# Moving one weight split to VectorE and narrowing the last chunk by column halves in a graph-attention block

## The reference, cut to what matters

```
h   = relu(layernorm(x))                        # x: 2048 x 256
hs  = layer_norm(h) * ln1 ; ht = layer_norm(h_target) * ln1
q, k, v = ht @ Wq, hs @ Wk, hs @ Wv             # 8 heads of 32
probs = softmax(where(adj != 0, q @ k.T, -1e30)) # 2048 x 2048 for each head
ht  = ht + (probs @ v) @ Wo + bo
ht  = layer_norm(ht) * ln2                      # the "y" of the kernel
ff  = gelu(ht @ W1) @ W2                        # W1: 256 x 1024, W2: 1024 x 256
out = x + ht + ff
```

## Time and profile before

| | |
|---|---|
| runs shown | 508.99, 513.01, 1082.84 us; median 513.01 |
| profiled execution | 511.34 us, span of the core's instructions 509.7 us (1.64 us lie outside) |
| mean granted TensorE clock | 0.992 |
| busy | PE 476.3 us (93%), DVE 420.1 (82%), ACT 391.1 (77%), POOL 310.0 (61%) |
| stretches | attention until about 395 us, mixing until 406.6, feed-forward until 503.2, tail until 509.7 |

### The profile page before, as it was taken

The page is one execution under the profiler, slowest core; times in us unless marked ns, Lnnn a source line. Parts: engine busy times, 40 slices in busy tenths (PEclk is TensorE's granted clock), DMA queues, the critical chain, the costliest instruction groups (busy, mean ns, idle before and its releaser), DMA issues.

```text
span 509.7 us, 10621 instructions
## 1 busy us (share of the span) xinstructions
PE 476.3 (93%) x4364; PEld 244.4 (48%) x4364; DVE 420.1 (82%) x626; ACT 391.1 (77%) x467; POOL 310.0 (61%) x153
## 2 busy tenths in 40 slices
PE   3899979999999899999899999999999799999995
PEld 1466623333333333333333333333335688888884
DVE  5688589999998999999999999999997787565252
ACT  4787978998998898998899998899896371627250
POOL 1000009995997997998998999899999500000000
PEclk9899999999999999999999999999999999999999
DMA  8998399722642851322762400160000100202021
GB/s 255 246 205 151 89 250 402 251 42 51 201 78 38 119 123 37 70 42 44 90 164 42 86 1 2 32 181 1 2 1 2 44 11 33 84 0 84 0 84 44
DMA packets 53232, 46.95 MB, mean 92 GB/s; under 512 B 35454, under 2 KB 46108, under 8 KB 52668
## 3 DMA queue, kind: packets, MB, share of 16 engines
q1 hardware_dynamic: 50672, 37.30, 27.4%
q0 software_dynamic: 2480, 8.92, 10.1%
q10 hardware_dynamic: 28, 0.01, 0.0%
HBM read 31.93 MB, written 14.81 MB: 92 GB/s over the span
## 4 chain that ended last, share of the span: by engine, by line
PE 49%; ACT 18%; DVE 17%; issue 8%; POOL 4%; DMA 3%; DVEq 0%; POOLq 0%
DVE probs L994 11%; ACT probs L721 10%; PE acc L1335 9%; PE slot L1320 8%; ACT maskT L654 4%; PE acc L1353 4%; PE slot L1435 3%; PE slot L1433 3%; PE slot L1434 3%; PE acc L1450 3%; PE acc L1448 3%; PE acc L1449 3%; PE slot L1233 3%; PE slot L1251 2%; POOL added_up L528 2%
## 5 line engine op out<-in xcount | busy, mean ns | idle before, releaser
L994 DVE SCALAR_TENSOR_TENSOR probs<-maskT,slot 128x1024 f32<-128x1024 bf16 x256 | 298.8, 1217 | 14.9 <-PE slot L1320 14.4
L721 ACT ACTIVATE probs<-probs 128x1024 f32<-128x1024 f32 x256 | 261.1, 1053 | 21.9 <-DVE probs L994 11.0
L528 POOL TENSOR_TENSOR added_up<-added_up,probs 128x1024 f32<-128x1024 f32 x96 | 226.7, 2396 | 1.7 <-ACT probs L721 1.6
L1335 PE MATMUL acc<-probs,V 128*32 128x512 f32 x1024 | 137.2, 608 | 7.1 <-ACT probs L721 7.1
L1353 PE MATMUL acc<-probs,ones 128*32 128x256 f32 x1024 | 77.0, 379 | 0.0
L1320 PE MATMUL slot<-q_hi,k_hi 32*128 32x512 f32 x512 | 64.9, 496 | 7.6 <-DVE probs L994 7.6
L1353 PEld LDWEIGHTS acc<-probs,ones 128*32 128x32 f32 x1024 | 33.3, 110 | 72.8 <-issue 71.2
L525 POOL TENSOR_TENSOR added_up<-probs 128x1024 f32<-128x1024 f32 x16 | 38.0, 2391 | 44.5 <-ACT probs L721 24.4
L1320 PEld LDWEIGHTS slot<-q_hi,k_hi 32*128 32x128 f32 x512 | 24.6, 182 | 65.7 <-DVE probs L994 54.0
L781 ACT ACTIVATE g_full<-slot 128x512 f32<-128x512 f32 x32 | 19.2, 600 | 45.3 <-issue 30.8
L1320 PE MATMUL slot<-q_lo,k_hi 32*128 32x512 f32 x512 | 52.0, 392 | 0.0
(11 more groups left out here) (132 smaller groups left out, 512.2 us busy)
## 6 DMA issues: line engine op xcount, KB each, us to landing
adj_raw<-in_adj POOLq DMA_DIRECT2D x16, 512.0 KB, 5.3
xs<-in_x SPq DMA_DIRECT2D x4, 512.0 KB, 6.9
htn<-in_L_gnn_h_target SPq DMA_DIRECT2D x4, 512.0 KB, 7.0
ht_saved<-htn SPq DMA_DIRECT2D x1, 2048.0 KB, 7.6
k_hi_saved<-k_hi SPq DMA_DIRECT2D x1, 2048.0 KB, 10.6
k_lo_saved<-k_lo SPq DMA_DIRECT2D x1, 2048.0 KB, 14.1
v_saved<-V SPq DMA_DIRECT2D x1, 2048.0 KB, 9.4
inverse<-inverse_saved SPq DMA_DIRECT2D x8, 256.0 KB
```

Of the source, the lines that this page charges most:

```text
L528: nc.gpsimd.tensor_tensor(added_up[:, pair], added_up[:, pair], at(i), ALU.add).then_inc(added, 1)
L721: nc.scalar.activation(p, p, ACT.Exp).then_inc(exped, 1)
L994: nc.vector.scalar_tensor_tensor(out=probs[:, u % RING], in0=m, scalar=MASKED if c else CEILING, in1=slot[u % SLOTS][:], op0=ALU.add, op1= ...
L1335: mm = pe.matmul(acc[HD * j:HD * j + HD, 0, :], V[:, i, h * HD:(h + 1) * HD], probs[:, (PAIRS * k + j // 2) % RING, j % 2, :], start=(i == 0),
```

## The change

It has three parts.

1. The subtraction that makes `w2_lo` leaves POOL and becomes one DVE instruction, `split_second_weight`, right behind `y_apply(0)` and ahead of `add_residual(2)`.
2. POOL's last residual: its first step waited for the norm of chunk 0 (`norm_y`), its second for `yT_lo` of chunk 0 (`y_lo_out`). Both now stand behind `y_lo_out`.
3. The last chunk's narrowing becomes `narrow_last`: all eight blocks f for the columns 0 to 127 first, then all for 128 to 255. The first half is joined, transposed (into `slot[0]`, behind the fifth block of the second half) and finished while the second half runs; the second half is joined in two pieces of 256 rows, each transposed and finished by itself. SP waits for the counts that this gives.

```diff
--- before.py
+++ after.py
@@ -452,7 +452,7 @@
             for c in range(NCH):
                 for half in range(2):
                     ts = slice(half * TILES // 2, (half + 1) * TILES // 2)
-                    sp.wait_ge(summed, TILES * c + (half + 1) * TILES // 2)
+                    sp.wait_ge(summed, TILES * c + (half + 1) * TILES // 2 + (TILES if c == LAST else 0))
                     sp.dma_start(out_rows[:, rows_of(c), :][:, ts, :], result[:, ts, :]).then_inc(stored, 16)
                 if c < LAST:
                     sp.dma_start(xr[:], x_rows[:, rows_of(c + 1), :]).then_inc(x_again, 16)
@@ -569,12 +569,9 @@
                         nc.gpsimd.tensor_tensor(w1_lo[:], w1_raw, w1_hi[:].bitcast(F32), ALU.subtract
                                                 ).then_inc(w1_lo_made, 1)
 
-            pool.wait_ge(w2_hi_made, 1)
-            nc.gpsimd.tensor_tensor(w2_lo[:], w2_raw, w2_hi[:].bitcast(F32), ALU.subtract).then_inc(w2_lo_made, 1)
-
-            pool.wait_ge(norm_y, LN2)
+
+            pool.wait_ge(y_lo_out, DC)
             make_residual(LAST, 0)
-            pool.wait_ge(y_lo_out, DC)
             make_residual(LAST, 1)
 
             general = load_flag(pool, "pool")
@@ -1067,6 +1064,37 @@
                     nc.vector.scalar_tensor_tensor(out=result[:, t, :], in0=acc4[:, t, :], scalar=nodes[:, n:n + 1],
                                                    in1=xr[:, t, :], op0=ALU.mult, op1=ALU.add).then_inc(summed, 1)
 
+            def finish_last():
+                def join_part(d, at, width):
+                    ts = slice(at, at + width)
+                    nc.vector.tensor_tensor(out_T[:, d, ts], acc[:, d, ts], yT[LAST % 2][:, d, ts], ALU.add
+                                            ).then_inc(joined, 1)
+
+                def result_part(t, d):
+                    n, ds = LAST * TILES + t, slice(d * P, (d + 1) * P)
+                    nc.vector.scalar_tensor_tensor(out=result[:, t, ds], in0=slot4[0][:, t, ds], scalar=nodes[:, n:n + 1],
+                                                   in1=xr[:, t, ds], op0=ALU.mult, op1=ALU.add).then_inc(summed, 1)
+
+                dve.wait_ge(out_turned, 2 * LAST)
+                dve.wait_ge(narrowed, DC * LAST + 1)
+                join_part(0, 0, CHUNK)
+                dve.wait_ge(x_again, 16 * NCH)
+                dve.wait_ge(stored, 32 * LAST)
+                dve.wait_ge(out_turned, 2 * LAST + 1)
+                for t in range(TILES):
+                    result_part(t, 0)
+                dve.wait_ge(narrowed, DC * NCH)
+                for half in range(2):
+                    join_part(1, half * CHUNK // 2, CHUNK // 2)
+                for half in range(2):
+                    dve.wait_ge(out_turned, 2 * LAST + 2 + half)
+                    for t in range(half * TILES // 2, (half + 1) * TILES // 2):
+                        result_part(t, 1)
+
+            def split_second_weight():
+                dve.wait_ge(w2_hi_made, 1)
+                nc.vector.tensor_tensor(w2_lo[:], w2_raw, w2_hi[:].bitcast(F32), ALU.subtract).then_inc(w2_lo_made, 1)
+
             def divide_last():
                 dve.wait_ge(inverses_in, 16 * GROUPS * NCH)
                 dve.wait_ge(context_out, GROUPS * NCH)
@@ -1088,6 +1116,7 @@
             y_stats(0)
             y_root(0)
             y_apply(0)
+            split_second_weight()
             add_residual(2)
             turned_y_lo(0)
             add_residual(1)
@@ -1115,10 +1144,11 @@
                     find_largest()
                 else:
                     make_flag()
-                join(c)
+                if c < LAST:
+                    join(c)
                 if c == 0:
                     add_residual(LAST)
-            finish(LAST)
+            finish_last()
 
             general = load_flag(dve, "dve")
             with dve.If(general):
@@ -1435,6 +1465,28 @@
                         mm = pe.matmul(dst, w1_lo[:, d, fs], yT_hi[:, d, :], start=False, stop=(d == DC - 1))
                     mm.then_inc(widened, 1)
 
+            def narrow_last():
+
+                pe.wait_ge(summed, TILES * LAST)
+                for d in range(DC):
+                    for f in range(FC):
+                        pe.wait_ge(gelu_lo, LAST * FC + f + 1)
+                        ds, dst = slice(d * P, (d + 1) * P), acc[:, d, :]
+                        pe.matmul(dst, w2_hi[:, f, ds], g_hi[:, f, :], start=(f == 0), stop=False)
+                        pe.matmul(dst, w2_hi[:, f, ds], g_lo[:, f, :], start=False, stop=False)
+                        mm = pe.matmul(dst, w2_lo[:, f, ds], g_hi[:, f, :], start=False, stop=(f == FC - 1))
+                        if d == 1 and f == FC // 2:
+                            pe.wait_ge(joined, DC * LAST + 1)
+                            for t in range(TILES):
+                                turned_mm = pe.transpose(slot4[0][:, t, 0:P], out_T[:, 0, t * P:(t + 1) * P], ident[:])
+                            turned_mm.then_inc(out_turned, 1)
+                    mm.then_inc(narrowed, 1)
+                for half in range(2):
+                    pe.wait_ge(joined, DC * LAST + 2 + half)
+                    for t in range(half * TILES // 2, (half + 1) * TILES // 2):
+                        mm = pe.transpose(slot4[0][:, t, P:D], out_T[:, 1, t * P:(t + 1) * P], ident[:])
+                    mm.then_inc(out_turned, 1)
+
             def narrow(c):
                 if c == 0:
                     pe.wait_ge(w2_lo_made, 1)
@@ -1470,10 +1522,12 @@
                 else:
                     pe.wait_ge(largest_made, 2 * NCH + 1)
                     pe.transpose(slot[2][0:1, 0, 0:P], largest_all[:], ident[:]).then_inc(largest_turned, 1)
-                narrow(c)
+                if c < LAST:
+                    narrow(c)
+                else:
+                    narrow_last()
                 if c == 0:
                     attend(LAST)
-            turn_out(LAST)
 
             general = load_flag(pe, "pe")
             with pe.If(general):
```

## The result

The changed kernel takes 506.36 us in the median of 18 executions, the one before 511.33 of 18. The ratio of the undisturbed executions is 0.9916 with a 95% interval of 0.9893 to 0.9939, which is 4.3 us less (3.1 to 5.5). The forecast was 508.1 us, 3.3 less. Executions that a disturbance made far longer than the rest (here 1082.84 us of before and 512.75 of the changed kernel) stay in the medians of this document and are left out of its ratios.

What follows compares the result with a forecast made beforehand. PE bounds the feed-forward, with a DVE wait chain ahead of it and a tail behind the last matmul; 2.8 + 0.46 = 3.3 us off 511.34 gives 508.1 us, range 505.5 to 510.6.

Steps and rivals of the forecast that it cites:

- The wait at L1017: DVE's norm of chunk 0, between attention and feed-forward: POOL's w2_lo holds L1017 2.93 us; removing it gains PE 2.8.
- The added DVE instruction: w2_lo subtraction on DVE behind y_apply(0): takes 2.28 us, hidden, with 0.3 us to spare before PE's widening.
- POOL's residual: Moved behind y_lo_out: may hold DVE's first g_lo by 0 to 0.97 us, within PE's room of 1.38; cost 0.
- The engines' part of the tail: Last chunk by column halves: 0.94 us less behind the last matmul, 0.48 more in the stream, gain 0.46.
- Rival D: Last chunk's narrowing: 24 matmuls in a row into one bank each cost more; 512.9 us at 0.1 each; chance 0.02.
- The DMAs behind it: From the last result to the end of the span: 3.27 us, assumed unchanged.
- signs of being wrong: PE idling before the first widening or its block 7, last-chunk matmuls over 0.23 us apart, end DMAs over 3.3.
- 0.2 if the transfers queue: End of kernel: if the two final transfers queue behind each other, the tail's gain is 0.2 us.
- a measurement could tell only about 10 us from no change: Whole kernel: measurement can tell about 2%, 10 us, from no change; faster 0.02, within 0.96, slower 0.02.
- B: Ahead of PE's widening: DVE's w2_lo runs 4.53 us, or POOL's hold exceeds 1.38 us; 510.0 us; chance 0.07.
- C: L1017's hold was not POOL's instruction, so only the tail is won; 510.9 us; chance 0.03.
- A: Tail gives nothing or takes a little: 128-column results cost as much as 256, or two DMAs queue; 508.6 us; chance 0.12.

Runs made afterwards that it cites:

- e3: Kernel before with one more wait: POOL's w2_lo subtraction stays on POOL but runs behind the first norm; 510.66 us, ratio 0.9974 to before.
- e4: Whole change plus a second DVE instruction of 128x2048 with two SBUF inputs behind w2_lo; 509.39 us, ratio 0.9987 to before.
- e5: Whole change with POOL's first residual step waiting for the first norm again, its second for y_lo_out; 508.99 us, ratio 0.9957 to before.
- e2: Kernel before with part 3 alone, the last chunk by column halves, the split staying on POOL; 511.36 us, ratio 1.0016 to before.
- e1: Kernel before with parts 1 and 2 (split on DVE, later POOL residual) and the old tail; 506.62 us, ratio 0.9898 to before.
- look4: Fourth of four more profiles of the unchanged kernel before; first widening 12.29 us behind the start of attend(2), against 10.59 in its first profile.

## Why the prediction was right

**The wait at L1017** (2.93 us, of which PE could take 2.67 to 2.83, I took 2.8). Measured 2.83 at the first turn and 2.89 at the first widening. That it was POOL's instruction is shown by e3, where one wait on POOL removes it.

**The added DVE instruction** (2.28 us, hidden, 0.3 to spare). Measured 2.29, hidden, with about 0.6 to spare (e4).

**POOL's residual** (cost 0; a hold of 0 to 0.97 on the first `g_lo`, room 1.38 at PE). Measured a hold of 0.89, no idle time on PE. The row of the trace left open whether instructions with two SBUF inputs are held; e3 and e5 show it, in both directions. Leaving the residual where it was would have cost 0.47.

**The engines' part of the tail** (0.94 less behind the last matmul, 0.48 more in the stream, 0.46 net). Measured 1.11 less behind it (3.23 to 2.12) and 0.44 to 0.5 more in the stream (the profiles' stream of 96.0 to 96.2 with the old tail varies by half as much), 0.6 to 0.7 net. Rival D's price, for many matmuls in a row into one bank, is nil: they stay 0.23 apart.

**The DMAs behind it.** This step failed: "The DMAs behind (506.43 to 509.70, 3.27) I leave as they are." They took 4.34, 1.0 more than in the old tails, which is one of the signs of being wrong that the forecast had named, and took back what the engines had won; the bound that I did give, 0.2 if the transfers queue, was too small and on the wrong side of zero. From the start of the last matmul to the end are 7.0 us in the mean of the nine profiles with the old tail and 6.9 in the four with the new one, and the stream costs 0.5 more: part 3 is a loss of about 0.4 us by the profiles, and e2's time (0.8 more, -0.7 to +2.4) agrees.

**What the sum lacked.** The gap on PE cost more than its length, since the clock fell behind it in four of six profiles. I read only one profile of before, and that was one of the two without the fall. 2.9 + 1.1 - 0.4 = 3.6 us is what the stages give, inside the measured 3.1 to 5.5; the other 0.7 of the 4.3 is not accounted for. The forecast's 3.3 has the right size for part 1 and two misses, 1.1 us for the clock and 0.9 for the tail (0.46 gained forecast, 0.4 lost found), that nearly cancel. That they do is luck, and so is that the one profiled execution of 511.34, at a scatter of 2 us each way, fell on the median of 511.33. That a measurement could tell only about 10 us from no change was too coarse: eighteen executions of each gave 4.3 us to 1.2 either way.

Rivals B and C are excluded by the rows and e3: the subtraction took 2.29 us, PE never idled behind it, and L1017's hold went with POOL's instruction. A, that the tail gives nothing or takes a little, is what happened, through the DMAs that it named second. No version here is shown to beat the whole change: e1, which lacks part 3, has the lowest ratio, 0.9898, with an interval that holds the whole change's.

## What to carry to other kernels

Where a tiny VectorE instruction is long once, look at what GpSimd was doing and when it ended; then move that work to a place where nobody holds or is held, which on GpSimd may not exist, and count each VectorE instruction with two SBUF inputs near it. Read several profiles of the kernel before, with the granted clock of each stretch: here an idle stretch of 2.6 us on PE was followed by another 1.65 us of loss in some executions and not in others. Where executions scatter, set their times against their mean clocks before explaining a difference of a few us. At the end of a kernel count up to the last byte stored: two stores that are issued closer together may end no earlier.

## What I had not expected of the hardware

- A gap of 2.6 to 2.7 us on a busy PE was followed by the lower clock in four of six profiles (0.50 in the windows of 402 to 404 us, in look4 of 404 to 406, full again by 406 to 408), which cost 1.65 us; one of 4.87 us by 0.50 for about 6 us, which cost 3.0. Behind 1.29 us (e4) it stayed at 1.00.
- The scatter of before, 505.8 to 513.1 us in the 60 undisturbed executions, follows the mean granted clock: 0.980 at the upper end, 1.000 near the lower.
- The hold works both ways: GpSimd's step of 2.4 us took 4.35 when it started 0.15 us behind a VectorE subtraction of 2.28 us.
- Instruction fetches fall into the last stores of a kernel (3 in the last 5 us, 16, 8 and 16 KB), and the stores ended with a thin run of about 1.2 us at some 8 to 25 GB/s where they followed each other closely.
